# Keys' half first in the first and last group's rotation, the last group's norm ahead of the shared sums, and GpSimd's ids in four steps

## What is computed

```python
h = concat(tokens(x), txt)
n = ln(h)                                    # attention
q, k = split(elu(n @ Wqk + bqk) + 1)         # 8 heads of 16
q_r, k_r = rope(q), rope(k)                  # t * cos + concat(-t2, t1) * sin
z = 1 / (q . mean(k) + 1e-6)
h = h + (q_r @ (k_r^T v / 193)) * z + conv3(n)
xt = ln(h)                                   # experts
shared = (silu(xt @ sw1) * (xt @ sw3)) @ sw2
scores = xt @ gate_w.T
idx = top_k(scores + biases, 2)
p = sigmoid(top_k(scores, 2)); p = p / sum(p)
y_e = (silu(xt @ w1[e]) * (xt @ w3[e])) @ w2[e]
out = h + sum_k p_k * y_idx_k + shared
```

## Time and profile before

| | |
|---|---|
| median of three runs | 247.2 us |
| profiled execution | 247.54 us, of which the span is 245.7 |
| busy PE / DVE / ACT / POOL | 219.6 / 186.5 / 157.5 / 131.7 us |
| share of PE, DVE, ACT, POOL | 89%, 76%, 64%, 54% |
| instructions | 5601 |

### The profile page before, as it was taken

The page is one execution under the profiler, slowest core; times in us unless marked ns, Lnnn a source line. Parts: engine busy times, 40 slices in busy tenths (PEclk is TensorE's granted clock), DMA queues, the critical chain, the costliest instruction groups (busy, mean ns, idle before and its releaser), DMA issues.

```text
span 245.7 us, 5601 instructions
## 1 busy us (share of the span) xinstructions
PE 219.6 (89%) x1477; PEld 188.4 (77%) x1485; DVE 186.5 (76%) x711; ACT 157.5 (64%) x429; POOL 131.7 (54%) x178
## 2 busy tenths in 40 slices
PE   2868898989899999978989979999999999999970
PEld 2757787979798989856666657888888888888760
DVE  2547799998989898998987867666666666666774
ACT  3044786687768686868964165777777777777540
POOL 1300000338778787778767711666666666666710
PEclk9999999999999999999999999999999999999997
DMA  6999974051516101010112421414323333338397
GB/s 187 345 349 357 328 252 194 0 207 58 207 54 210 56 15 54 11 43 24 54 45 66 122 58 33 121 45 131 82 79 95 86 93 85 88 85 240 110 297 197
DMA packets 31566, 31.75 MB, mean 129 GB/s; under 512 B 4338, under 2 KB 27419, under 8 KB 30768
## 3 DMA queue, kind: packets, MB, share of 16 engines
q1 hardware_dynamic: 26824, 24.40, 33.4%
q0 software_dynamic: 3392, 6.38, 8.0%
q10 hardware_dynamic: 1320, 0.61, 0.9%
HBM read 22.83 MB, written 9.06 MB: 130 GB/s over the span
## 4 chain that ended last, share of the span: by engine, by line
PE 57%; DVE 23%; issue 6%; ACT 6%; SPq 3%; DMA 3%; DVEq 0%; ACTq 0%
PE bank L1668 16%; PE bank L1688 10%; PE bank L1677 5%; DVE att L954 3%; DVE att L947 3%; DVE st L888 3%; DMA xp_both<-in_patches 3%; PE bank L1586 2%; PE bank L1380 2%; PE bank L1657 2%; PE bank L1463 2%; PE bank L1449 2%; PE bank L1571 2%; PE bank L1574 2%; DVE hrow L996 2%
## 5 line engine op out<-in xcount | busy, mean ns | idle before, releaser
L870 POOL DMA_INDIRECT y_dram<-att,goal x56 | 55.8, 996 | 36.8 <-ACT att L766 36.2
L859 POOL DMA_INDIRECT xs_dram<-xd,pos_i x50 | 49.8, 995 | 23.6 <-issue 18.6
L1380 PE MATMUL bank<-wt,xp_both 128*128 128x128 f32 x288 | 39.9, 291 | 7.2 <-DMA xp_both<-in_patches 7.1
L1380 PEld LDWEIGHTS bank<-wt,xp_both 128*128 128x128 f32 x288 | 37.6, 204 | 8.8 <-DMA xp_both<-in_patches 5.7
L1688 PE MATMUL bank<-w_sb,att 128*128 x224 | 34.6, 277 | 0.0
L1296 DVE CAST xsT_h<-bank 128x128 fp32r<-128x128 f32 x56 | 16.3, 291 | 24.1 <-PE bank L1657 23.0
L752 ACT ACTIVATE att<-bank 128x256 f32<-128x256 f32 x56 | 21.5, 383 | 18.8 <-PE bank L1668 18.8
L1688 PEld LDWEIGHTS bank<-w_sb,att 128*128 128x128 f32 x224 | 29.4, 191 | 0.4 <-issue 0.2
L1668 PE MATMUL bank<-xp_both,xsT_h 128*128 x56 | 26.7, 478 | 0.7 <-DVE xsT_l L1298 0.7
L1309 DVE TENSOR_TENSOR att<-att,bank 128x256 f32<-128x256 f32 x56 | 23.2, 414 | 1.6 <-ACT att L752 1.6
L766 ACT ACTIVATE att<-bank,goal 128x128 f32<-128x128 f32 x56 | 20.6, 367 | 4.8 <-PE bank L1688 0.7
(11 more groups left out here) (224 smaller groups left out, 506.8 us busy)
## 6 DMA issues: line engine op xcount, KB each, us to landing
xp_both<-in_patches SPq DMA_DIRECT2D x6, 1152.0 KB, 5.0
xs_all<-xs_dram SPq DMA_DIRECT2D x56, 65.0 KB, 1.8
xd<-y_dram SPq DMA_DIRECT2D x8, 384.0 KB, 5.3
w<-in_w SPq DMA_DIRECT2D x2, 1024.0 KB, 11.0
y_dram<-att,goal POOLq DMA_INDIRECT x56, 2.4
xs_dram<-xd,pos_i POOLq DMA_INDIRECT x50, 2.3
xp_both<-in_patches SPq DMA_DIRECT2D x1, 768.0 KB, 5.6
hrow<-in_txt SPq DMA_DIRECT2D x2, 384.0 KB, 8.0
```

The source lines that it names most:

```text
L859: nc.gpsimd.indirect_dma_start(out=xs_dram[:, :], out_offset=bass.IndirectOffsetOnAxis(ap=pos_i[0:rows, j, k:k + 1], axis=0), in_=xd[0:row ...
L870: nc.gpsimd.indirect_dma_start(out=y_dram[:, :], out_offset=bass.IndirectOffsetOnAxis(ap=goal[u][:, 0:1].bitcast(I32), axis=0), in_=ys[u][ ...
L1380: M(ps[:, 0:D], xp[p][:, k, :], wt[:, k, :], start=(k == 0), stop=False)
```

## The change

The edits:

- **First and last group's rotation.** `turn_parts` and `turn` are replaced by `half_parts` and `half_turn`, called for the keys' half first and then for the queries' half. `turned_at` gives each wait its count. In the last group `heads` stands between the queries' parts and their addition. On PE `sums` of the last group stands ahead of `turn_turned`, which moves behind a `shared_up`.
- **Loop.** `patch_rows` of the next group goes ahead of `turn`. `positions` moves from the end of an iteration into the next one, behind `mixed`.
- **Last groups on ACT and DVE.** `rstd2` and `norm2` of group 6 go behind `inverse` of group 7; the first Silu and its table load go behind the scores of group 6. On DVE the last group's norm, its three rows of `xd` and the places and positions of group 6 go ahead of the shared additions and products. The remainders and products that follow are dealt out anew.
- **GpSimd.** `goals` has four steps for both choices at once instead of five; the ids come from a wider table. The power in `shares` is gone: DVE makes the reciprocal in `positions`, so POOL's last step waits for DVE and DVE's reciprocal for POOL's sum.

```diff
-WEIGHED = 7
+WEIGHED = 6
+SUMMED = 5
...
+    flat = np.broadcast_to(flat, ids.shape)
+    return np.concatenate([ids.reshape(P, 2 * J), np.full((P, 1), BIG), flat.reshape(P, 2 * J)], 1).astype(np.int32)
...
+        def turned_at(g, at):
+            return g + (1 if g == 0 else 2) + (1 if at == 0 and g in (0, G - 1) else 0)
...
             turned_queries(G - 1)
-            rstd2(G - 2)
             chances(G - 3)
             key_sums(G - 1)
-            norm2(G - 2)
             inverse_log(G - 1)
             inverse(G - 1)
+            rstd2(G - 2)
+            norm2(G - 2)
             columns2(G - 2)
...
-                then_pool(nc.gpsimd.tensor_tensor(crossed[:], chosen[:, :, 0], chosen[:, :, 1], ALU.subtract))
+                then_pool(nc.gpsimd.tensor_tensor(crossed[:], chosen[:], chosen[:, :, ::-1], ALU.subtract))
                 then_pool(nc.gpsimd.tensor_scalar(apart[:], crossed[:], 0.0, float(NID), ALU.is_gt, ALU.mult))
-                nc.gpsimd.tensor_tensor(xd[:, at, 0, D].bitcast(I32), ids[:, at, 0], apart[:], ALU.add)
-                nc.gpsimd.tensor_tensor(xd[:, at, 1, D].bitcast(I32), ids[:, at, 1], apart[:], ALU.subtract)
+                nc.gpsimd.tensor_tensor(xd[:, at, :, D].bitcast(I32), ids[:, at, :], apart[:], ALU.add)
...
-                then_pool(nc.gpsimd.tensor_tensor(odds_sum[:], odds_sum[:], minus[:], ALU.pow))
-                then_pool(nc.gpsimd.tensor_tensor(xd[:, at, :, D + 1], odds[:, :, ::-1], odds_sum[:].rearrange(
+                pool.wait_ge(pos_done, 2 * g + 1)
+                then_pool(nc.gpsimd.tensor_tensor(xd[:, at, :, D + 1], odds[:, :, ::-1], odds_part[:].rearrange(
...
+            def half_parts(g, at):
+                dve.wait_ge(fta_done, g + 1)
+                dve.wait_ge(ftb_done, g + 1)
+                f, s, o = (x[:, :, at:at + D].rearrange("p t (h a e) -> p t h a e", a=2, e=HD // 2) for x in (ft, sinx, ss))
+                for a in range(2):
+                    V.tensor_tensor(o[:, :, :, a], f[:, :, :, 1 - a], s[:, :, :, a], ALU.mult)
+                V.tensor_tensor(cc[:, :, at:at + D], ft[:, :, at:at + D], cosx[:, :, at:at + D], ALU.mult).then_inc(cs_done, 1)
+            def half_turn(g, at):
+                dve.wait_ge(cs_done, turned_at(g, at))
...
+                V.tensor_tensor(rr[:, :, at:at + D], cc[:, :, at:at + D], ss[:, :, at:at + D], ALU.add).then_inc(rr_done, 1)
...
+                if g < EARLIER:
+                    dve.wait_ge(pool_chain, WEIGHED * g + SUMMED)
+                    V.reciprocal(odds_part[:], odds_sum[:]).then_inc(pos_done, 1)
...
                 turn_parts(i)
+                patch_rows(i + 1)
                 turn(i)
-                patch_rows(i + 1)
                 patch_stats(i + 1)
-                if i >= 2:
-                    positions(i - 2)
...
+            mean2(G - 2)
             remainder_w13(0)
+            attended(G - 1)
+            mixed(G - 1)
             positions(G - 3)
...
-            pe.wait_ge(rr_done, G)
-            turn_turned(G - 1)
             sums(G - 1)
             shared_up(0, 1)
+            turn_turned(G - 1)
             attend(G - 1)
```

More of the change, by code:

```diff
@@ L687, in _ @@
             turned_queries(G - 1)
-            rstd2(G - 2)
             chances(G - 3)
             key_sums(G - 1)
-            norm2(G - 2)
             inverse_log(G - 1)
             inverse(G - 1)
+            rstd2(G - 2)
+            norm2(G - 2)
             columns2(G - 2)
+            act.wait_ge(s_done, G)
+            nc.scalar.copy(s_col[:].rearrange("p (g b) -> p g b", b=2), s_all[:, :, 0:2]).then_inc(s_done, 1)
+            scores(G - 2)
             act.preload_act_table(ACT.Silu)
             shared_silu(0, 0)
-            scores(G - 2)
-            act.wait_ge(s_done, G)
-            nc.scalar.copy(s_col[:].rearrange("p (g b) -> p g b", b=2), s_all[:, :, 0:2]).then_inc(s_done, 1)
             shared_silu(0, 1)
-            round_w13(3)
             act.preload_act_table_set("natural_log_exp_and_others")
@@ L715, in _ @@
             shared_silu(1, 1)
-            shared_silu(2, 0)
-            round_w13(4)
+            round_w13(3)
             act.wait_ge(nm2_done, G)
@@ L938, in elu_rest @@
                                        op0=ALU.min, op1=ALU.max).then_inc(ftb_done, 1)
+            def half_parts(g, at):
[7 more added lines that the diff above has]
+                dve.wait_ge(cs_done, turned_at(g, at))
+                after(dve, kv_done, g)
+                after(dve, qrT_done, g)
+                V.tensor_tensor(rr[:, :, at:at + D], cc[:, :, at:at + D], ss[:, :, at:at + D], ALU.add).then_inc(rr_done, 1)
             def turn_parts(g):
@@ L1100, in _ @@
             elu_rest(0)
-            turn_parts(0)
-            turn(0)
+            half_parts(0, D)
+            half_turn(0, D)
+            half_parts(0, 0)
+            half_turn(0, 0)
             dve.wait_ge(s_cols, 32)
@@ L1130, in _ @@
                     mixed(i - 1)
+                if i >= 3:
+                    positions(i - 3)
                 if i == 2:
@@ L1180, in _ @@
             mixed(G - 2)
+            positions(G - 4)
             elu_most(G - 1)
             elu_rest(G - 1)
-            turn_parts(G - 1)
+            half_parts(G - 1, D)
+            half_turn(G - 1, D)
             second_rows(G - 2)
-            turn(G - 1)
+            half_parts(G - 1, 0)
+            heads(G - 1)
+            half_turn(G - 1, 0)
             second_stats(G - 2)
-            heads(G - 1)
+            tap_behind(G - 1)
+            places(G - 3)
             mean2(G - 2)
-            tap_behind(G - 1)
             remainder_w13(0)
-            places(G - 3)
+            attended(G - 1)
+            mixed(G - 1)
             positions(G - 3)
             remainder_w13(1)
-            attended(G - 1)
-            mixed(G - 1)
-            remainder_w13(2)
             second_rows(G - 1)
@@ L1205, in _ @@
             choices(G - 2)
-            shared_add(0)
-            shared_mul(1, 0)
             dve.wait_ge(rs2_done, G)
@@ L1212, in _ @@
             last.then_inc(nm2_done, 1)
-            shared_mul(1, 1)
-            places(G - 2)
-            positions(G - 2)
             dve.wait_ge(nm2_done, G)
@@ L1221, in _ @@
             last.then_inc(x2_done, 1)
-            remainder_w13(3)
+            places(G - 2)
+            positions(G - 2)
+            shared_add(0)
+            shared_mul(1, 0)
+            shared_mul(1, 1)
             shared_mul(2, 0)
+            remainder_w13(2)
+            choices(G - 1)
             shared_mul(2, 1)
-            remainder_w13(4)
-            shared_add(1)
-            choices(G - 1)
             places(G - 1)
@@ L1230, in _ @@
             V.tensor_tensor(tab_p[:], bank[6][:, TOTAL_AT:TOTAL_AT + E], cst[:, C_BASE:C_BASE + E], ALU.add).then_inc(ends_done, 1)
+            shared_add(1)
+            remainder_w13(3)
+            shared_mul(3, 0)
             shared_add(2)
-            shared_mul(3, 0)
+            remainder_w13(4)
             shared_mul(3, 1)
@@ L1616, in _ @@
             shared_down(0)
+            place(G - 2)
             shared_up(2, 0)
-            place(G - 2)
+            turn_second(G - 1)
             shared_up(2, 1)
+            gate(G - 1)
             shared_down(1)
-            turn_second(G - 1)
-            gate(G - 1)
-            shared_down(2)
             shared_up(3, 0)
             place(G - 1)
+            shared_down(2)
             shared_up(3, 1)
```

30 lines of the change are left out of this document (15 added, 15 removed).

## The result

The changed kernel takes 255.53 us (median of four runs, 255.26 to 256.1) against 247.08 of the kernel before (four runs); the ratio on record is 1.0361, 95% interval 1.0329 to 1.0392. The forecast was 254.1 with a range of 251.5 to 257.0. The profiled run took 255.26 us, its span 253.1.

What follows compares the result with a forecast made beforehand. Bound: a last-ending chain over TensorE (57%) and VectorE (23%), shared branch racing scatters to the expert loop's start. Terms -0.2 (first group), -0.9 (groups 1 to 6), +8.0 (last group on) gave 6.9: 247.2 to 254.1 us, range 251.5 to 257.0.

Steps and rivals of the forecast that it cites:

- The stall at `mean2`: VectorE, last group: waits 2.8 us for ScalarE's scale of group 6, made behind the inverse; second_rows(7) 2.9 later.
- The order behind it: Behind second_rows(7): choices(7) after the third shared product starts at 133.1, not 128.42; shared_up(3, 1) 7.2 us later.
- Rival 1: Tail behind second_rows(7) catches up, only the 2.9 us of second_rows is left: 250.1 us; chance 0.15.
- Rival 2: Faster: ScalarE has group 6's scale when VectorE reaches mean2, nothing stalls: 246.1 us or a little less; chance 0.05.
- The halves of the last rotation: Last group: kst at 109.8, not 111.67, but whole rotation at 111.2, not 110.15; ScalarE's key sums at 112.3, not 111.87.
- The walk: Step-by-step times of the new order up to the expert loop's first transposition: 153.3 instead of 146.39.
- The loop: Groups 1 to 6: patch rows ahead of the rotation's last addition gain 0.15 us a group, 0.9 in all.
- Rival 3: More: TensorE idles between 111.9 and 117.5, its clock falls, matmuls up to second_rows take twice as long: 257.0; chance 0.14.
- GpSimd at nothing: GpSimd saves 6.6 us, nothing booked; scatters end 4.3 later, at 146.4, and stay hidden with 4.30 to spare.

Runs made afterwards that it cites:

- norm_back: The changed kernel with ScalarE's rstd2 and norm2 of group 6 put ahead of group 7's inverse again; 254.16 us, ratio to before 1.0275.
- choices_first: The changed kernel with one VectorE line moved: choices(7) ahead of shared_mul(2, 0); 252.84 us, ratio to before 1.0243.
- down2_back: The changed kernel with shared_mul(2, 1) and shared_add(1) ahead of choices(7), shared_down(2) ahead of shared_up(3, 0) and place(7); 254.0 us, ratio to before 1.0256.
- both_back: The changed kernel with group 6's norm ahead of the inverse again and before's lists from second_rows(7) on; 249.54 us, ratio to before 1.0067.
- loop_free: The kernel before with the loop's edits, GpSimd's steps and the first group's halves, positions(5) behind mixed; 247.33 us, ratio to before 0.9994.
- patch_only: The kernel before with one loop edit, the next group's patch rows ahead of the rotation's last step; 247.96 us, ratio to before 1.0035.
- swap_only: The kernel before with two loop edits: next patch rows ahead of turn, positions moved into the next iteration; 250.18 us, ratio to before 1.0142.
- patch_ids: The kernel before with next patch rows ahead of turn and GpSimd's ids in one addition instead of two; 245.27 us, ratio to before 0.993.

## Why the prediction was right

**The stall at `mean2`: right.** VectorE sat 2.95 us there, 2.8 were forecast, and `norm_back` shows that the end pays for it.

**The order behind it: right, and the larger part.** `choices(7)` behind the third shared product was booked with +4.7 at its start; it came 3.72 later than in before, in a walk that ran 1.4 us late by then (`second_rows(7)` at 120.0 instead of 118.59). From `second_rows(7)` to `choices(7)` it took 13.55 us, 13.1 were walked. `choices_first` shows one of the two places in its time and its trace, `down2_back` the other in its time alone. Rival 1, catching up, is refuted: nothing is caught up behind `second_rows(7)`. Rival 2 did not occur: `mean2` was not fed in time.

**The halves of the last rotation: right.** The walk had the key sums on ScalarE 0.43 later than in before, in a rotation that starts 0.9 sooner, so 1.33 later in spite of the earlier `kst`; the pair `both_back` and `loop_free` shows 1.37 from the same ELU.

**The loop: mis-sized.** Booked were 0.9 for groups 1 to 6 and 0.2 for the first, less 0.2 for a reciprocal. The last ELU came 2.24 sooner. Of this 0.71 is no gain, for the first group's ELU, ahead of every edit, was that much sooner (before, then the changed kernel):

```profile
19.84 0.69 DVE L931 SCALAR_TENSOR_TENSOR att<-att,bank 128x512 f32<-128x512 f32 x1 [1.25 <-ACT att L495]
```
```profile
19.13 0.69 DVE L934 SCALAR_TENSOR_TENSOR att<-att,bank 128x512 f32<-128x512 f32 x1 [1.24 <-ACT att L500]
```

From there to the ELU of group 1 the kernels need 12.36 and 12.30 us: the first group's halves gave 0.06 and not 0.2. Between the ELU of group 1 and that of group 7 the kernel before needs 73.67 us, the changed one 72.20 and `patch_only` 72.11: 0.25 for each of six groups, the whole wait of the earlier trace rows and not 0.15 of it. The swap alone gives it, and its trace shows that wait no more. The reciprocals cost nothing that shows. So of the 1.3 us by which the walk is too late at every step up to `second_rows(7)`, some 0.6 are gains booked too small and 0.7 the early start of this execution; the differences between steps hold to 0.2.

**The clock: the rival's mechanism came, and the forecast had left it out.** Rival 3 saw TensorE's idle times ahead of `second_rows` and priced them at 2.9. The granted clock did fall there, but off the path; it fell a second time, where the walk had not looked, and there `shared_down(2)` paid 1.33. From `second_rows(7)` to the loop's start the changed kernel needs 35.44 us, the walk had 33.3: beside the 1.33, 0.45 lie ahead of `choices(7)`, and some 0.3 behind `shared_up(3, 1)`, where the walk had a wait filled. That the walk met the measured loop start to 0.7 us is thus in part luck: 2.1 too little lost here stand against 0.6 too little gained in the loop and an execution that began 0.71 early. Counted from the first group's ELU the loss was 8.35, and the walk had 6.9.

**GpSimd at nothing: right for this change, but for the wrong margin.** The last scatter ends at 145.43, 8.6 us ahead of the loop. But the 4.30 that I let the scatters spare are not spare: from the last scatter's end to the first transposition the runs show 3.23 to 3.34 us where the transposition waits for them. Before has 1.0 to spare, not 4.30. `positions` moved an iteration later delays GpSimd's first scatter by 4.35, and GpSimd's shorter steps pay that back (the last scatter ends at 144.82 in `swap_only`, at 141.84 in `loop_free`, which also has the first group's halves). In the changed kernel the later tail hides all of it; in a kernel whose loop leads, as `swap_only`, `patch_only` and `patch_ids`, it decides.

## What to carry to other kernels

Before moving a step behind another on one engine's list, name the engine that waits for the moved step and what is queued behind that wait: here one scale behind an inverse and one product ahead of a routing step cost 2 to 3 us each. A second chain that ends 4 us early is not 4 us of slack; subtract the transfer that lies between its end and its use. When a lead on the main chain does not arrive at the end, look for the chain that was second: 0.19 us saved six times on GpSimd turned a loss of 0.35% into a gain of 0.7%.
